# A generator chunk in two halves, and the adapter steps moved: a fused sequence kernel on one core

## The reference

```python
# layer 0
scale = cond @ norm_w.T + 1.0
h = x * (scale[:, None, :] * rsqrt(mean(x * x) + EPS))
val, gate = split(h @ up_w.T)                 # 2 x 1024 columns
h = val * gelu(gate)
x = act_quant(h) @ weight_quant(down_w).T + x  # row-wise 8 bits, ternary weights
# layer 1, the adapter: its weights are made for each sequence
dWd = ((cond @ Wdd.T + bdd) * 0.1).reshape(B, 128, 256)
dWu = ((cond @ Wdu.T + bdu) * 0.1).reshape(B, 256, 128)
down = relu(x @ (Wd + dWd).T + bd)
out = x + down @ (Wu + dWu).T + bu
```

## Time and profile before

| | |
|---|---|
| median of 3 runs | 525.67 us (521.31 to 526.25) |
| the profiled execution | 522.1 us, span 520.3 us |
| TensorE busy | 468.8 us (90%) |
| VectorE, ScalarE, GpSimd busy | 403.8 (78%), 365.0 (70%), 227.2 us (44%) |
| granted TensorE clock, mean | 0.978 |
| HBM traffic | 45.8 MB, 88 GB/s over the span |

### The profile page before, as it was taken

How to read it: one execution, slowest core, us unless ns; L and a number is a source line. 1 busy time by engine, 2 the same in 40 slices (tenths; PEclk the granted TensorE clock), 3 DMA queues, 4 the chain that set the end, 5 groups by cost and what they waited for, 6 DMA issues and landing times. The chain is left out here.

```text
span 520.3 us, 9822 instructions
## 1 busy us (share of the span) xinstructions
PE 468.8 (90%) x3206; PEld 263.2 (51%) x3206; DVE 403.8 (78%) x832; ACT 365.0 (70%) x632; POOL 227.2 (44%) x569
## 2 busy tenths in 40 slices
PE   2677988898898999999999999999999999999863
PEld 1234554454555545555555555555555555555442
DVE  3589889998998778778778768877877778887731
ACT  4579777976886777776776877767777666677631
POOL 0164245325433126546445445445454444444355
PEclk9999999998999999999999999999999999999957
DMA  7856866585552444555565545565555446553442
GB/s 249 331 103 197 191 189 156 160 225 177 149 162 59 87 100 104 120 141 130 130 136 131 126 111 131 142 122 132 137 97 143 108 107 113 122 122 72 102 116 76
DMA packets 120402, 71.64 MB, mean 138 GB/s; under 512 B 104672, under 2 KB 105376, under 8 KB 118176
## 3 DMA queue, kind: packets, MB, share of 16 engines
q1 hardware_dynamic: 120352, 71.02, 54.3%
HBM read 37.44 MB, written 8.39 MB: 88 GB/s over the span
## 5 line engine op out<-in xcount | busy, mean ns | idle before, releaser
L674 PE MATMUL bank<-up_hi,xs_hi 128*128 128x512 f16 x512 | 154.0, 383 | 11.3 <-DVE hid L555 6.0
L414 ACT ACTIVATE gel<-bank,rms 128x512 f32<-128x512 f32 x128 | 87.2, 682 | 98.7 <-PE bank L674 89.9
L674 PE MATMUL bank<-up_hi,xs_lo 128*128 128x512 f16 x512 | 153.7, 382 | 0.0
L674 PE MATMUL bank<-up_lo,xs_hi 128*128 128x512 f16 x512 | 153.7, 382 | 0.0
L555 DVE SCALAR_TENSOR_TENSOR hid<-bank,rms,gel 128x512 f32<-128x512 f32 x128 | 95.4, 745 | 15.8 <-ACT gel L414 14.9
L419 ACT ACTIVATE hid<-hid,amax 128x1024 f32<-128x1024 f32 x64 | 73.2, 1144 | 26.3 <-DVE amax L569 26.1
L350 POOL TENSOR_TENSOR ad_lo<-adapt,ad_hi 128x256 f16<-128x256 f32 x64 | 41.6, 670 | 110.4 <-DVE ad_hi L601 110.4
L674 PEld LDWEIGHTS bank<-up_lo,xs_hi 128*128 128x128 f16 x512 | 50.4, 98 | 61.6 <-issue 2.1
L674 PEld LDWEIGHTS bank<-up_hi,xs_lo 128*128 128x128 f16 x512 | 50.4, 98 | 61.4 <-issue 1.6
L563 DVE TENSOR_REDUCE amax<-hid 128x1 f32<-128x1024 f32 x64 | 78.1, 1220 | 2.2
L674 PEld LDWEIGHTS bank<-up_hi,xs_hi 128*128 128x128 f16 x512 | 48.6, 99 | 48.7 <-issue 12.5
(11 more groups left out here) (65 smaller groups left out, 629.0 us busy)
## 6 DMA issues: line engine op xcount, KB each, us to landing
xT_s<-in_xT SPq DMA_DIRECT2D x32, 256.0 KB, 3.1
xn_s<-in_xn SPq DMA_DIRECT2D x32, 256.0 KB, 3.2
stage<-in_WddT SPq DMA_DIRECT2D x8, 1024.0 KB, 6.1
stage<-in_WduT SPq DMA_DIRECT2D x8, 1024.0 KB, 5.1
out<-out_s SPq DMA_DIRECT2D x32, 256.0 KB, 2.4
adapt<-in_up_wT SPq DMA_DIRECT2D x4, 512.0 KB, 6.3
x<-in_down_wT SPq DMA_DIRECT2D x1, 1024.0 KB, 12.7
qT<-qn SPq DMA_TRANSPOSE x64, 3.1
```

What stands on the lines that cost most here:

```text
L414: nc.scalar.activation(gel[:, c], u_gate[c][:], ACT.Gelu, scale=rms[:, t // TPB % XN_SLOTS, t % TPB:t % TPB + 1]).then_inc(gelu_done, 1)
L674: ins = nc.tensor.matmul(dst[:], a[:, t // TPB % 2, k, cols], w[:, c, k, v, :], start=(k == 0 and n == 0), stop=(k == KD - 1 and n == 2))
```

## The change

Four things change together.

1. `generate(q)` becomes `generate(q, n)`: the first half of chunk s - 1 stands between `down` and `up(s, 1)`, the second behind `up(s, 1)`. The first half waits only for VectorE's part of the subtraction, the second for GpSimd's too. On VectorE the first half is evacuated in the same step, behind the residual and `total`; the second is the first thing in the next step. `rsqrt_guess` moves from the start of the odd step to behind this evacuation (and stays there in the steps that have none).
2. `pool_cols` for q >= 2 goes from 1152 to 1024, the second half exactly; VectorE subtracts 1024 columns and not 896.
3. `ADAPT` is earlier: 19, 21, 22, 23, 25, 26, 27, 29, ... (four steps for three sequences) until it meets 2b + 7, and 64, 65, 67 for the last three. The program has three steps fewer.
4. `split_tiles`: a tile of x1 is split no earlier than in the step that makes it, t + 3. From tile 36 on it is split in just that step. Only for s == NT `quantize(s - 1)` stands behind `residual_high`.

```diff
-END = NT + 9
+END = NT + 6
 def adapter_step(b):
-    if b >= B - 4:
-        return (NT + 1, NT + 2, NT + 3, NT + 5)[b - B + 4]
-    return max(2 * b + 10, NGEN + 4 + (3 * b + 1) // 2)
+    if b >= B - 3:
+        return (NT, NT + 1, NT + 3)[b - B + 3]
+    return max(2 * b + 7, NGEN + 3 + (4 * b + 2) // 3)
...
-    return [2 * b + i for b in range(B) for i in range(TPB) if ADAPT[b] - 4 + i == s]
+    return [t for t in range(NT) if max(ADAPT[t // TPB] - 4 + t % TPB, t + DOWN) == s]
...
-    return 768 if q < 2 else 1152
+    return 768 if q < 2 else CHUNK // 2
...
-                if 0 <= s - 1 < NT:
-                    quantize(s - 1)
+                    if s > 0:
+                        quantize(s - 1)
                 for t in split_tiles(s):
                     residual_high(t)
+                if s == NT:
+                    quantize(s - 1)
...
             for s in range(END):
-                if s % TPB == 1 and s // TPB + 1 < B:
-                    rsqrt_guess(s // TPB + 1)
+                if 2 <= s < NGEN + 2:
+                    evacuate(s - 2, 1)
                 if s < NT:
                     gate(s, 0)
...
                 for b in sequences(s, -2):
                     total(b)
-                if 2 <= s < NGEN + 2:
-                    evacuate(s - 2, 0)
-                    evacuate(s - 2, 1)
+                if 1 <= s < NGEN + 1:
+                    evacuate(s - 1, 0)
+                if s % TPB == 1 and s // TPB + 1 < B:
+                    rsqrt_guess(s // TPB + 1)
...
-            def generate(q):
+            def generate(q, n):
                 pe.wait_ge(w_lo_v, q + 1)
-                pe.wait_ge(w_lo_p, q + 1)
+                if n == 1:
+                    pe.wait_ge(w_lo_p, q + 1)
...
                     down(s - DOWN)
+                if 1 <= s < NGEN + 1:
+                    generate(s - 1, 0)
                 if s < NT:
                     up(s, 1)
                 if 1 <= s < NGEN + 1:
-                    generate(s - 1)
+                    generate(s - 1, 1)
```

More of the change, by code:

```diff
@@ L686, in down @@
                 ins.then_inc(y_full, 1)
-            def generate(q):
+            def generate(q, n):
                 pe.wait_ge(w_lo_v, q + 1)
-                pe.wait_ge(w_lo_p, q + 1)
[L691 to L700, removed]
+                if n == 1:
+                    pe.wait_ge(w_lo_p, q + 1)
+                after(pe, gen_done, 2 * q + n - 2)
+                for m in range(BCH):
+                    dst = gen_ps[(2 * q + n) % 3][:].rearrange("p (h m b) -> p m h b", h=2, m=BCH)[:, m]
+                    cols = slice((n * BCH + m) * P, (n * BCH + m + 1) * P)
+                    passes = ((0, cdiag_hi), (0, cdiag_lo), (1, cdiag_hi))
+                    for k, (part, moving) in enumerate(passes):
+                        ins = nc.tensor.matmul(dst, wsplit[:, q % 2, part, cols], moving[:],
+                                               start=(k == 0), stop=(k == len(passes) - 1))
+                ins.then_inc(gen_full, 1)
             def middle(b):
```

## The result

The changed kernel takes 536.31 us (median of 4 runs, 533.19 to 538.66) against 525.35 us for the kernel before in the same comparison: ratio 1.022 with a 95% interval of 1.017 to 1.026. It is slower, by some 11 us, and inside the range of the forecast, near its upper end. Its profiled execution has a span of 532.4 us (before 520.3), so 12.1 us of span are to be explained.

What follows compares the result with a forecast made beforehand. TensorE was taken to bound the long middle. Terms 0 + 2.0 + 4.8 + 6.6 - 1.6 - 3.5 = +8.3 on 522.1 us gave 530.4, 534.0 at the median; 532 was taken, range 518 to 539, the forecast's own 527 to 537.

Steps and rivals of the forecast that it cites:

- the two late waits: After the generator: `output` waiting for middle_low, +4.8 us, and gelu of the next even step waiting for rms, +6.6 us.
- The generator: Steps 1 to 16: the first generator half newly waits for VectorE's subtraction; pair 17.35 against 17.59 us, in all about 0.
- Work moved: Earlier adapters put one `middle` and two `output` groups more before the end of up(63,1): 3 x 0.65 = +2.0 us.
- `output` waits for `middle_low`: Every fourth catch-up step (22 to 42): TensorE waits 0.8 us for GpSimd's middle_low, six times, +4.8 us.
- g: Start of gelu(s,1) in an even step, from which times are counted: guess forecast at 6.95 us, middle_low at 13.9.
- Late pairs: Pairs of steps, 45 to 62: a loop through rms, gelu and residual takes 14.15 against TensorE's 13.42 us; +6.6 us.
- The rule of the Trainium skill: VectorE instructions with two SBUF inputs and GpSimd instructions reading SBUF exclude each other; late pair some 14.3 us, +1.4.
- Old waits: Steps 17 to 63: some 2.6 us of the old kernel's TensorE waits come off, about 1 stays: -1.6 us.
- The end: From gelu(63,1): last total at 23.4 against 27.5 us, -4, with ScalarE some 0.5 behind: -3.5 us.
- rival 1: Faster, 521.5 us: GpSimd's chain stays off the path; a guess 0.8 earlier removes the +4.8 and +6.6; chance 0.2.

## Why the prediction was right, and where it was off

The forecast, slower by the two late waits and a generator that stays as it was, held: 536.3 for 532, within the forecast's own range of 527 to 537. On the span the sum said +8.3 and the trace says +12.1. The mechanism was right; that the number stayed inside the range was in part luck. The waits came to 6.5 us more than forecast, and 2.0 at the end and 0.7 in the first stretch went the other way; without these two the time would be some 539, outside. 1.7 of the first stretch are the kernel before's loss of clock and no doing of the change.

1. **The generator**, forecast about 0 (even 9.47, odd 7.88): 9.46 and 7.85, the stretch to step 16 -1.0, and the mark of step 16 -0.7 with the start in it. Without the kernel before's loss of clock it would be +0.7: -1.7 in six pairs, +1.3 up to step 3 (forecast 1), +1.1 in step 16 (forecast 0.3). The guess started 3.06 us after VectorE's subtraction (forecast 3.1) at 0.16. The subtraction ended at 101.38 and TensorE's first matmul of the half began at 101.43: the handover that the prediction put at 0.06 is 0.05. Two runs show the mechanism: moving the guess alone gives the 8.9 us, and lengthening the subtraction by 0.26 lengthens each step by 0.26 or 0.27. One input was off without harm: GpSimd's subtraction of 1024 columns took 2.63 (at 100.74), not 2.3, since it began while VectorE was still at its own (last section).
2. **Work moved**, forecast +2.0: 468.9 busy for 468.8; as groups, +3.3 before step 45, -1.3 behind it.
3. **`output` waits for `middle_low`**, forecast 0.8 in every four steps, +4.8: this is the term that was mis-sized. It was 1.6 (29.75 - 28.14) in each of the four groups whose wait is 1.40 to 1.44, and there were eight waits, of 0.38 to 1.64, 9.1 in all. With the one of 1.13 in step 18, for the `gate` behind the late root of the guess in step 17, waits in the catch-up came to +10.1. I had used the late pairs' order for the catch-up. There, adapters fall in even steps too, and adapter_high stood between xs_lo and gate (254.99 in the trace above): 0.40 that I had struck out, and the guess came at g + 7.30, not 6.95. GpSimd's small steps (there are twelve to a root, not eleven) were the other half: one took 0.37, beginning while VectorE was at adapter_high, one 0.48, beginning with VectorE's low half of x1 (263.13), and 0.19 to 0.20 otherwise; the chain took 3.65 for 3.2. Together `middle_low` was ready at g + 14.7 for 13.9, and since nothing in this loop had slack, the 0.8 doubled the wait.
4. **Late pairs**, forecast 14.15: 14.25. The links, from gelu(e,1): the root ready at 10.74 (10.65), gelu 10.78 (10.7), gate 11.50 (11.42), residual 12.46 (12.39), high half 12.98 (12.9), gelu again 14.25. The 0.1 is again the first small step, 0.37. What the sum left out: TensorE waits in these pairs before `output`, 0.66 or 0.67 in most of them, and its rows show no other wait. `middle_low` hangs on the same root. The links above come to 14.25 without TensorE, so this wait follows from the loop and doesn't lengthen it. The rule of the Trainium skill (SBUF — State Buffer, Who interferes with whom) that I weighed gave some 14.3 for another reason, a low half of x1 held up by adapter_low. The trace has no such block here: L593 started at 453.65, 0.03 before adapter_low, and took 0.41, and it was GpSimd's adapter_low that was long in such a pair (two instructions, 1.53 at 439.43, for 1.29 to 1.30). By the rule whichever starts first holds the port; the trace agrees, and only the order that I assumed was wrong. The 2.34 of the earlier trace rows that the prediction put beside the rule is of an instruction with one input, and so bears on the exclusion but not on the form with two; the 0.81 of the earlier trace rows does.
5. **Old waits**, -1.6: with 3 and 4 together, 9.8 forecast net and 16.3 measured, nearly all of the difference in the catch-up.
6. **The end**, forecast -3.5: -5.5. The transpose of x1(61) let `middle` start at 10.7 and not at 11.5, so down(63) ended at 13.8 and not at 14.6; the residual began at once, and x1(63) was done at 14.3, not 15.4. What follows took 7.6 for 8.0. The 0.5 that I gave ScalarE for lateness did not show. (Four `middle` are left behind up(63,1), not the three that the prediction names; its 3 x 0.65 has it right.)

Two statements of the prediction fell. I took 532 in place of the sum's 534 because a wait once taken should leave slack; in loops this tight it does not. And rival 1 was weighed as though the guess had only to be 0.8 earlier for both waits to vanish. The runs show the guess worth 10 us at the front, but a second hold-up, the splits, then kept the late pairs at 14.21. In the sum I had put both into one loop and so could not see that it closes in two ways, each nearly enough by itself.

What stays open: what of the 7.9 us in the generator is due to the halves and what to their place and to the larger share of VectorE; why the stores of the outputs come late in some groups of the catch-up and not in others; and whether the early adapter table is worth anything by itself.

## What to carry to other kernels

- Moving one small instruction out of the way of another engine's long one was worth 9 us (1.7 of them a loss of clock that went with it); a structure built around it, with an added dependence of each step on the step before, gave nearly all of it back. Try the move alone first.
- An instruction that starts another engine's chain belongs early, however small it is and however idle that engine looks (GpSimd was busy half the time): what counts is the distance from the end of the chain to who waits for it, in each kind of step apart, and sums made for one kind don't hold for another that has one more instruction.
- When two waits cover the same time, taking away either shows little (1.9 and 1.5 us), and both together 5.7: a fix without effect isn't yet a wrong theory.

## What was not expected of the hardware

TensorE's granted clock fell in the midst of the generator, right behind waits of some 2 us. In the run with 1280 columns on VectorE TensorE waited 2.08 us in every odd step from 3 on. After three of these waits the granted clock was at 0.50 for some 3.4 us (in windows of 1 us from 85 on it was 0.92, 0.50, 0.50, 0.50, 0.88), and the step took 1.7 us more; after the same wait in the other odd steps (at 104.50, for one) it stayed at 1.00. In the changed kernel the wait is 1.81 in odd steps from 3 on and none of these steps shows a loss. The kernel before has such a place too, after a wait of 1.70. Windows of the kernel before there:

```profile
120.00:122.00 2.00, 0.30 (x11) 0.18 (x8) 1.90 (x5) 2.00 (x3) 1.45 (x8) 1.00 0.89 188
122.00:124.00 2.00, 2.00 (x27) 1.39 (x28) 1.97 (x3) 0.77 (x1) 1.74 (x5) 0.56 0.94 363
```

That step took 10.32 where its like take 8.65. Nor did the clock fall behind a wait of 3.35 in step 2 of the run with 1280 columns (at 39.58; 1.00 from 39 to 45). So the wait's length alone doesn't decide; what else does stays open. The cost is plain: 0.26 more in 14 steps would have been 3.7 us, and the three losses of 1.7 put 5.1 on top (the stretch grew by 8.0, since it also began 0.8 shorter).

And the two subtractions of one chunk did not run side by side where they overlapped. GpSimd's took 2.63 for 1152, for 1024 and for 768 columns (99.04 before, 100.74 changed, 103.33 with 1280 columns on VectorE). VectorE was still at its own for the first 0.39, 0.64 and 1.11 us of that. Without these it is 2.24, 1.99 and 1.52, in step with the columns: GpSimd did nothing until VectorE was through, an inference from these three rows. So columns moved from GpSimd to VectorE brought GpSimd's end forward by little: from the start of VectorE's subtraction it came after 3.31 us in the kernel before, 3.20 in the changed one and 2.99 with 768 columns on GpSimd.
